# A binarised 3x3 convolution behind a group norm on one core: thresholds moved to GpSimd, and row sums stored without their two zero columns

## The reference

```python
# x: 32 x 56 x 56 x 32 (NHWC), W: 3 x 3 x 32 x 32, beta, v, bias: 3 numbers each
xn = (x - mean(x over H, W)) / sqrt(var(x over H, W) + 1e-5)        # per image and channel
B[m] = sign(W - mean(W) + u[m] * std(W)),  u = -1, -0.5, 0, 0.5, 1
alpha = solve(Bf.T @ Bf, Bf.T @ wf);  W_eff = sum over m of alpha[m] * B[m]
out = 0
for n in range(3):
    A = sign(clip(xn + v[n], 0, 1) - 0.5)
    out += beta[n] * (conv3x3_same(A, W_eff) + sum(alpha) * bias[n])
return x + out
```

## Time and profile before

| | us |
|---|---|
| median of three runs (lowest, highest) | 194.65 (194.5, 195.14) |
| the profiled execution, device time | 194.47 |
| its span in the profile | 192.7 |
| PE busy, share of the span | 174.0, 90% |
| DVE busy | 163.3, 85% |
| ACT busy | 154.2, 80% |
| POOL busy | 55.1, 29% |

### The profile page before, as it was taken

One profiled execution on the slowest core, in us unless ns is written; L12 is line 12 of the kernel. 1 busy time (PEld: TensorE's weight loads), 2 busy tenths in 40 slices (PEclk: granted clock), 3 DMA queues, 4 the chain that ended last, 5 costly groups with the idle time before them and its releaser, 6 DMA issues.

```text
span 192.7 us, 4809 instructions
## 1 busy us (share of the span) xinstructions
PE 174.0 (90%) x1828; PEld 133.8 (69%) x1828; DVE 163.3 (85%) x409; ACT 154.2 (80%) x221; POOL 55.1 (29%) x72
## 2 busy tenths in 40 slices
PE   1898988749999999999899989999989999999992
PEld 1687765634868787868677777878777857677671
DVE  5579995999999999999988999899999899975242
ACT  2719968998898989999998989998988898872131
POOL 6264010006060606060605051323232242434000
PEclk9999999997999999999999999999999999999999
DMA  5999990063598989799988798989883837677725
GB/s 160 246 236 241 250 229 18 2 173 99 146 226 248 237 282 243 231 227 301 254 263 235 227 252 252 231 253 250 259 242 112 236 100 201 177 211 210 224 76 167
DMA packets 20476, 39.60 MB, mean 206 GB/s; under 512 B 9078, under 2 KB 9302, under 8 KB 20454
## 3 DMA queue, kind: packets, MB, share of 16 engines
q1 hardware_dynamic: 20144, 39.27, 74.8%
q10 hardware_dynamic: 310, 0.04, 0.1%
HBM read 13.15 MB, written 12.85 MB: 135 GB/s over the span
## 4 chain that ended last, share of the span: by engine, by line
PE 59%; DVE 18%; DMA 11%; ACT 7%; issue 2%; SPq 2%; DVEq 0%
PE conv_ps L843 33%; PE y_ps L876 10%; DMA s_odd<-s_even 10%; PE x_ps L795 6%; DVE raw_stats L629 5%; ACT signs L372 3%; DVE y_nat L620 3%; PE conv_ps L851 3%; DVE s_even L682 3%; PE conv_ps L846 2%; ACT x_ch L367 1%; ACT w_parts L413 1%; SPq L225 1%; ACT filt L410 1%; PE conv_ps L931 1%
## 5 line engine op out<-in xcount | busy, mean ns | idle before, releaser
L843 PE MATMUL conv_ps<-s_even,w_mm 128*64 128x448 f16 (+1 forms) x576 | 104.3, 335 | 3.5 <-DMA s_odd<-s_even 2.5
L846 PE MATMUL conv_ps<-s_odd,w_mm 128*64 128x448 f16 (+2 forms) x576 | 104.4, 323 | 0.0
L372 ACT ACTIVATE signs<-x_ch,neg_thr 128x784 f16<-128x784 f32 x96 | 85.3, 939 | 0.5
L843 PEld LDWEIGHTS conv_ps<-s_even,w_mm 128*64 128x64 f16 x576 | 60.6, 110 | 31.8 <-issue 10.3
L846 PEld LDWEIGHTS conv_ps<-s_odd,w_mm 128*64 128x64 f16 x576 | 60.8, 111 | 0.1
L335 POOL TENSOR_SCALAR lo_part<-signs,ratio_lo 128x1568 f16<-128x1568 f16 x14 | 22.0, 1575 | 103.1 <-DVE half_hi L675 103.1
L385 ACT ACTIVATE y_ch<-conv_ps,y_scale 128x896 f32<-128x896 f32 (+1 forms) x31 | 28.3, 911 | 17.6 <-PE conv_ps L851 10.3
L620 DVE SCALAR_TENSOR_TENSOR y_nat<-y_ps,y_const,x_nat 112x1024 f32<-112x1024 f32 (+1 forms) x30 | 34.4, 1148 | 8.3 <-PE y_ps L876 8.0
L629 DVE BATCH_NORM_STATS2 raw_stats<-x_ch 128x6 f32<-128x448 f32 (+1 forms) x64 | 31.6, 554 | 0.8 <-ACT x_ch L367 0.8
L876 PE MATMUL y_ps<-ident,y_ch 128*112 128x128 f32 x210 | 29.0, 278 | 0.0
L795 PE MATMUL x_ps<-ident,x_nat 112*128 112x112 f32 x192 | 25.5, 277 | 2.1 <-DMA x_nat<-in_x 1.4
(11 more groups left out here) (126 smaller groups left out, 126.7 us busy)
## 6 DMA issues: line engine op xcount, KB each, us to landing
x_nat<-in_x SPq DMA_DIRECT2D x16, 448.0 KB, 5.9
out<-y_nat SPq DMA_DIRECT2D x16, 448.0 KB, 5.9
s_odd<-s_even SPq DMA_DIRECT2D x32, 203.0 KB, 3.4
s_odd<-s_even SPq DMA_DIRECT2D x32, 188.5 KB, 3.8
x_nat<-in_x SPq DMA_DIRECT2D x16, 336.0 KB, 4.8
out<-y_nat SPq DMA_DIRECT2D x15, 322.0 KB, 2.9
s_odd<-s_even SPq DMA_DIRECT2D x16, 29.0 KB, 3.3
x_nat<-in_x SPq DMA_DIRECT2D x16, 14.0 KB, 5.9
```

Of the source, the lines that this page charges most:

```text
L372: act.activation(signs[q % 2][:, n, :, a, :], x_ch[q % CH_SLOTS][:, :, a, :], ACT.Sign, bias=neg_thr[q % 2][:, n, a:a + 1]).then_inc(signe ...
L843: last = nc.tensor.matmul(low[:, 0:n * ROWS], wt, s_even[b][:, part, r0:r0 + 2 * n, t:t + H], start=first, stop=end)
L846: last = nc.tensor.matmul(high[:, 0:m * ROWS], wt, s_odd[b][:, part, r0:r0 + 2 * m, t:t + H], start=first, stop=end and not at_edge)
```

## The change

POOL computes the thresholds in a new `thresholds(q)`: five instructions (`var_eps`, `ratio_root`, `twice_dev`, and two of `neg_thr`), the first four of them each waited for by the next. DVE keeps only the reciprocal in `invert_root`, and ACT's two `neg_thr` instructions go. `weigh_low` is split: `weigh_low_first(q)` no longer waits for `half_made`, only for signs 1 of q and for `lo_made` of the pair before; `thresholds(q + 1)` follows, and then `weigh_low_second(q)`. Rows of `s_even` and `s_odd` are 56 long; the middle tap goes first and writes all 56 rows of an output, and the outer taps write 55 of them. The six instructions that clear the zeros go.

```diff
-HP = H + 2
...
-        s_even = [sb(f"s_even{i}", [128, 2, 2 * BLOCKS, HP], FP16) for i in range(S_SLOTS)]
-        s_odd = [sb(f"s_odd{i}", [128, 2, 2 * BLOCKS, HP], FP16) for i in range(S_SLOTS)]
+        s_even = [sb(f"s_even{i}", [128, 2, 2 * BLOCKS, H], FP16) for i in range(S_SLOTS)]
+        s_odd = [sb(f"s_odd{i}", [128, 2, 2 * BLOCKS, H], FP16) for i in range(S_SLOTS)]
...
+            def begin_ratios():
                 link(ts(tmp[:, 5, 0:1], order[:, 0, 0:1], 0.0, 1.0, ALU.is_equal, ALU.mult))
                 tt(tmp[:, 5, 1:2], tmp[:, 5, 0:1], order[:, 0, 0:1], ALU.add).then_inc(divisor_ready, 1)
+
+            def split_ratios():
...
-            for b in range(S_SLOTS):
-                edge = s_even[b][:].rearrange("p s r h -> p (s r) h")
-                pool.memset(edge[:, :, 0], 0.0).then_inc(pads_ready, 1)
-                pool.memset(edge[:, :, HP - 1], 0.0).then_inc(pads_ready, 1)
-            pool.wait_ge(pads_ready, 2 * S_SLOTS)
+            def thresholds(q):
+
+                pool.wait_ge(moments_ready, 2 * (q + 1))
+                ts(var_eps[:], moments[q % 2][:, :, 1], GN_EPS, 1.0, ALU.add, ALU.mult).then_inc(pool_dev, 1)
+                pool.wait_ge(inverse_root, q + 1)
+                pool.wait_ge(pool_dev, 3 * q + 1)
+                tt(ratio_root[:], var_eps[:], inv_root[:], ALU.mult).then_inc(pool_dev, 1)
+                pool.wait_ge(pool_dev, 3 * q + 2)
+                tt(twice_dev[:], ratio_root[:], root[:], ALU.add).then_inc(pool_dev, 1)
+                pool.wait_ge(pool_dev, 3 * q + 3)
+                for a in range(2):
+                    ts(neg_thr[q % 2][:, :, a], order[:, 1, :], twice_dev[:, a:a + 1], moments[q % 2][:, a, 0:1],
+                       ALU.mult, ALU.add).then_inc(thr_ready, 1)
+                pool.wait_ge(thr_ready, 2 * (q + 1))
+
+            def weigh_low_first(q):
+                pool.wait_ge(lo_made, q)
+                pool.wait_ge(signed, 6 * q + 2)
+                ts(lo_part[0][:], signs[q % 2][:, 1].rearrange("p i a h -> p (i a h)"), ratio_lo[:, 0:1], 1.0,
+                   ALU.mult, ALU.mult).then_inc(lo_weighed, 1)
+
+            def weigh_low_second(q):
+                pool.wait_ge(half_made, q + 1)
+                ts(lo_part[1][:], signs[q % 2][:, 2].rearrange("p i a h -> p (i a h)"), ratio_lo[:, 1:2], 1.0,
+                   ALU.mult, ALU.mult).then_inc(lo_weighed, 1)
...
             order_beta()
+            begin_ratios()
+            thresholds(0)
             split_ratios()
             pool.wait_ge(ratios_ready, 3)
...
+            thresholds(1)
             pool.wait_ge(w_ready, 3)
...
+            thresholds(2)
             for q in range(2, PAIRS):
-                weigh_low(q)
+                weigh_low_first(q)
+                if q + 1 < PAIRS:
+                    thresholds(q + 1)
+                weigh_low_second(q)
...
             def begin_signs(q):
-                act.wait_ge(dev_ready, 2 * (q + 1))
-                if q == 0:
-                    act.wait_ge(order_ready, 3)
-                for a in range(2):
-                    act.activation(neg_thr[q % 2][:, :, a], order[:, 1, :], ACT.Identity,
-                                   bias=moments[q % 2][:, a, 0:1], scale=twice_dev[:, a:a + 1]).then_inc(thr_ready, 1)
                 act.wait_ge(thr_ready, 2 * (q + 1))
...
             def invert_root(q):
                 dve.wait_ge(root_ready, q + 1)
-                return mark(nc.vector.reciprocal(inv_root[:], root[:]))
-
-            def divide_variance(q, n):
-                dve.wait_ge(moments_ready, 2 * (q + 1))
-                settle(n)
-                return [mark(ts(twice_dev[:, a:a + 1], moments[q % 2][:, a, 1:2], GN_EPS, inv_root[:, a:a + 1],
-                                ALU.add, ALU.mult)) for a in range(2)]
-
-            def add_root(n):
-                for a in range(2):
-                    settle(n[a])
-                    ts(twice_dev[:, a:a + 1], twice_dev[:, a:a + 1], root[:, a:a + 1], None, ALU.add)\
-                        .then_inc(dev_ready, 1)
...
-                tt(inner(q, 0), rows(half_hi), signs[q % 2][:, 0].rearrange("p i a h -> p (i a) h"), ALU.add)\
+                tt(summed(q, 0), half_hi[:], flat(q, 0), ALU.add)\
...
-                tt(inner(q, 1), rows(lo_part[0]), rows(lo_part[1]), ALU.add).then_inc(lo_made, 1)
+                tt(summed(q, 1), lo_part[0][:], lo_part[1][:], ALU.add).then_inc(lo_made, 1)
...
-                    add_root(divide_variance(r, invert_root(r)))
+                    invert_root(r)
...
+            TAP_ORDER = [(1, 0, 2), (1, 0, 2), (0, 2, 1)]
+            TAP_OUT = [slice(1, H), slice(0, H), slice(0, H - 1)]
+            TAP_IN = [slice(0, H - 1), slice(0, H), slice(1, H)]
...
-                        for t in range(TAPS):
-                            first, end = i == 0 and t == 0, i == 2 and t == TAPS - 1
+                        for k, t in enumerate(TAP_ORDER[i]):
+                            first, end = i == 0 and k == 0, i == 2 and k == TAPS - 1
                             wt = w_mm[:, kind, t].rearrange("p o c -> p (o c)")
-                            last = nc.tensor.matmul(low[:, 0:n * ROWS], wt,
-                                                    s_even[b][:, part, r0:r0 + 2 * n, t:t + H],
+                            to, at = TAP_OUT[t], TAP_IN[t]
+                            last = nc.tensor.matmul(low[:, :, to], wt, s_even[b][:, part, r0:r0 + 2 * n, at],
                                                     start=first, stop=end)
-                            last = nc.tensor.matmul(high[:, 0:m * ROWS], wt,
-                                                    s_odd[b][:, part, r0:r0 + 2 * m, t:t + H],
+                            last = nc.tensor.matmul(high[:, 0:2 * m, to], wt, s_odd[b][:, part, r0:r0 + 2 * m, at],
                                                     start=first, stop=end and not at_edge)
                             if at_edge:
                                 we = w_edge[:, kind, t].rearrange("p o c -> p (o c)")
-                                last = nc.tensor.matmul(high[:, m * ROWS:n * ROWS], we,
-                                                        s_odd[b][:, part, r0 + 2 * m:r0 + 2 * n, t:t + H],
+                                last = nc.tensor.matmul(high[:, 2 * m:2 * n, to], we,
+                                                        s_odd[b][:, part, r0 + 2 * m:r0 + 2 * n, at],
```

31 lines of the change are left out of this document (11 added, 20 removed).

## The result

The changed kernel takes 196.45 us (median of 20 runs, 195.18 to 198.71). The kernel before, run beside it 20 times, took 195.21 (193.18 to 198.46). The ratio of the runs is **1.0081, 95% interval 1.0052 to 1.011**: slower by 0.8%, where 192.2 us and a gain had been predicted. The ratios here leave out, for each kernel, the runs that are more than 1.5% above its fastest, and the medians have all runs, so the two differ a little. The profiled execution took 195.18, with a span of 193.4.

What follows compares the result with a forecast made beforehand. PE was taken as the bound, with the chain add_x, statistics, sum_high, copy up to 0.9 us longer in some steps. Terms -0.84 - 1.1 - 0.15 - 0.2 + 0.3 - 0.25 + 0 = -2.25 from 194.47 gave 192.2 us; range 189.8 to 195.2.

Steps and rivals of the forecast that it cites:

- Columns: PE's convolutions: outer taps with 55 of 56 columns save 0.07 us a pair, over 12 pairs -0.84 us.
- The second scaling lands on the sums: Main part: POOL's second scaling starts at E + 1.3 and excludes DVE's sum; sum_high ends 0.27 us earlier, not 0.66.
- DVE level with PE: Main part: with weigh_first excluded by the first scaling, DVE's cycle is 9.6 us beside PE's 9.60, with no cover left.
- Copy waits: Main part: PE's four waits for a copy shrink 0.27 each, -1.1 us; the `spread_stats` wait -0.15, smaller early gaps -0.2.
- the rival of the copies: Main part: copies queue longer behind loads and stores and land as late as before; 193.3 us, or 194; chance 13%.
- Step -1: Setup: pair 2's thresholds come late behind four long DVE instructions, against DVE's shorter chain; 0, between -0.7 and +0.6 us.
- DVE's shorter chain, 0.66: Step -1: DVE's chain to `spread_stats`, for which PE waited, is 0.66 us shorter, set against ACT's loss of 0.8 to 1.6.
- Ends: Last steps: pair 14's low copy is late, +0.3 us (0 to 0.7); pair 15's sum_low comes earlier, -0.25.
- The gain of 0.25 for pair 15: End: pair 15's first scaling no longer waits for sum_half, so sum_low comes 1 us or more earlier: -0.25 us.
- The rival that ended slower: Main part: excluded instructions start afresh at POOL's end, so DVE's cycle of 10.1 us becomes the bound; 196.0 us; chance 20%.

Runs made afterwards that it cites:

- cols_only: The kernel before with only the zero columns, the rows of 58 and the tap order changed; thresholds and scalings as before: 194.27 us, 0.9937.
- pair2_15_old: The changed kernel with the thresholds of pairs 2 and 15 made by DVE and ACT as before: ratio 0.9951 to the kernel before.
- experiment 7: The changed kernel and `cols_only`, each without the f = 0 stores (columns 1 to 32 of each pair's output): 1.0049 and 0.9878 to the kernel before.
- pair15_old: The changed kernel with pair 15's thresholds alone made by DVE and ACT as before: ratio 1.0019 to the kernel before.
- swap_12: The changed kernel with pair 14's second scaling put ahead of pair 15's thresholds on POOL: 196.62 us, 1.0078 to the kernel before.
- cols_warm_15: `cols_only` with 14 unused matmuls ahead of step -1's gather and pair 15's first scaling released once its input is there: 193.16 us, 0.9926.
- after_warm: The changed kernel with 18 matmuls of unused results ahead of the gather of step -1: 196.77 us, 1.0084 to the kernel before.
- thr_only: The changed kernel with the zero columns and rows of 58 put back: 197.58 us, 1.0111 to the kernel before.
- cols_stats_first_warm: `cols_only` with pair 3's statistics ahead of pair 1's low scalings and sums, and 14 unused matmuls ahead of the gather, in step -1: 193.33 us, 0.9893.

## Why the prediction was wrong

**Columns (-0.84): right.** 9.67 became 9.60, and `cols_only` is 0.63% faster (0.21 to 1.04), 1.2 us of 195.2.

**The second scaling lands on the sums: right as a mechanism.** E + 1.51 (predicted 1.3, bound 1.5), weigh_first 1.03 (up to 1.0), steps of 9.60, DVE level with PE and not over it. The Trainium skill, SBUF — State Buffer, section Who interferes with whom, says that VectorE and GpSimd hold their shared interface for a whole instruction; the rows of the main part agree, weigh_first and the 24 columns of `spread_stats` (0.81 for 0.18) among them. Two scalings of the end stood still for a DVE instruction that was issued after them; the last section has them.

**Copy waits (-1.1, and -0.35 of smaller ones): not there.** sum_high ended at E + 3.98, 0.12 before, not 0.27, since every link was 0.05 to 0.2 longer than taken. And the waits did not shrink with it: 2.2 us beside 2.5 in the earlier trace rows, 3.5 in pair2_15_old. pair2_15_old against cols_only, 0.9951 against 0.9937, shows no worth of the new order in the main part: 0.14% slower, give or take 0.58, which leaves room for a gain of 0.9 us and not for the 1.45 predicted. In this the rival of the copies was nearer. Why the waits stayed is open; that other traffic makes the copies late is suggested by experiment 7, not shown.

**Step -1 (0, between -0.7 and +0.6): the step that failed first.** It costs 0.70%, 1.4 us, above its bounds, though the interval, 0.5 to 2.3 us, just reaches them. The lateness of the thresholds was right: they ended at 38.46, predicted 37.6 to 38.4. What I then did was to set DVE's shorter chain, 0.66, against it. That credit was void. `gather_lanes(3)` also waits for ACT's copy_in(4, 0), queued behind the signs. The copy and `spread_stats` before, then `spread_stats` after:

```profile
39.39 0.91 ACT L367 ACTIVATE x_ch<-x_ps 128x896 f32<-128x896 f32 x1
40.93 0.18 DVE L639 TENSOR_TENSOR spread_stats<-lane_mask,lane_stats 128x24 f32<-128x24 f32 x1
...
40.23 0.18 DVE L653 TENSOR_TENSOR spread_stats<-lane_mask,lane_stats 128x24 f32<-128x24 f32 x1
```

Before, the copy ended at 40.30 and `spread_stats` at 41.11, so ACT had 0.81 of slack. After, `spread_stats` is ready 0.7 earlier, at 40.41, and the copy ends at 41.98. I had followed to the engine which the wait named, and had not asked what else the gather waits for and how close behind it comes.

**Ends (+0.3 - 0.25): the step that failed next.** It costs 0.62%, 1.2 us (0.3 to 2.2 with the interval; the traces from S12 to S15 show 0.85 beside `pair15_old`). sum_low(14) at E + 4.7 was predicted and came at E + 4.72; before it was E + 3.64, not the 3.8 that I had read. But I priced only its copy. Queued behind sum_low are, on DVE, add_x(12, 1) and both scalings of pair 15, and on POOL pair 15's first scaling, which waits for it. The latter then fell on weigh_second (1.56 for 0.62) and took 2.80. So sum_high of pair 15 ended at 175.46, E + 11.12, where before it was E + 10.02. There is a second way, and I had not priced it either: the thresholds of pair 15 are late for ACT. Its signs, before and after:

```profile
165.49 1.79 ACT L372 ACTIVATE signs<-x_ch,neg_thr 128x784 f16<-128x784 f32 x2
...
166.41 1.79 ACT L395 ACTIVATE signs<-x_ch,neg_thr 128x784 f16<-128x784 f32 x2 [2.28 <-POOL neg_thr L333]
```

That is E + 1.50 and E + 2.07. weigh_second waits for signs 2, which ACT makes after these (at 168.07 before, at 169.00 after), and not for DVE's queue: it is issued 0.57 us later, at E + 6.47 instead of 5.90. So about half of the 1.10 us may be this wait, and the rest the exclusion. `pair15_old` takes both away, and weigh_second is back at E + 5.90. `swap_12` takes only the exclusion away (0.63 us for weigh_second) and makes the wait longer, E + 7.71; it loses as much. The gain of 0.25 for pair 15 isn't seen either (`cols_warm_15`).

Measured term by term: columns -1.2, step -1 +1.4, end +1.2, the rest +0.2, together the 1.6 us of 0.81%. Each has an interval of 0.8 to 1.0 us either way, and the rest is what is left over, not measured by itself. (The terms of the prediction add up to -2.24, which changes nothing.) The rival that ended slower had another mechanism, DVE as the bound of the main part. It did not happen, and that its 196.0 us came near the measured time is luck.

## What to carry to other kernels

Small instructions moved to an engine that shares an interface cost what their neighbour there holds, not their own length: look at every place in the program for what runs beside them, the first and the last steps above all, since they lack the cover of the steady ones. Before taking credit for a releaser that comes earlier, list all that the waiting instruction waits for and find the second to last. When a step is late, price everything queued behind it on each engine and not only its own output.

## What was unexpected of the hardware

POOL's two three-column instructions took 2.08 us in all beside two sums of DVE that follow each other closely, and 0.67 elsewhere. Even an instruction of two elements a partition took 0.84 beside sum_high, and 0.19 without it. In `after_warm` one such instruction, `twice_dev`, took 2.23 us: it started at 36.34 beside DVE's own low scaling, and ended at 38.57, just after the second of the two sums that follow that scaling (38.52).

How POOL's scalings of 2.29, 2.80 and 3.42 us came about is a pattern: each ended 1.44 or 1.45 after the end of a DVE instruction (sum_high at 174.01 of the earlier trace rows, and after the change weigh_first at 170.52 and sum_high at 175.46), so each ran almost whole behind it. But the last two were issued at 169.16 and 173.48 while DVE was at add_x, beside which other scalings run undisturbed (61.26, 1.57 long, above), and 0.7 and 1.0 us before that next DVE instruction. Why they had not begun is open; it wasn't tried.

The start of pair 0's convolution fell at 28.5 to 29.3 us in fourteen of the twenty profiled executions and at 30.6 to 31.5 in six (`thr_only` 31.15, `swap_12` 31.27, `cols_warm_15` 30.64 among them). The traces show what goes with it. In all six the granted clock was 0.50, the lower level, for 6.8 us, from 23.4 to 24.3 on. In the fourteen it was 1.00 throughout that stretch, except in `cols_stats_first_warm`, where it was 0.50 from 23.0 to 26.4 and the start fell at 29.02. In these seven executions PE had been busy for 0.8 us or less from 20 to 22 us, and in the thirteen others for 1.7 or more. What leaves PE idle there in some is open, and with one trace of each kernel it can't be said whether the kernel or the execution decides. It may be a part of why runs of one kernel lie between 193 and 199 us, and why 0.4% was hard to tell here.
